# Masking attention scores inside the PSUM banks instead of into an SBUF tile

## The reference, cut to what matters

```python
qkv = silu(hidden_states @ qkv_w.T)              # q, k, v of every head
scores = einsum('bhnd,bhmd->bhnm', cq, ck) * diag_decay      # inside blocks of 32 tokens
intra = einsum('bhnm,bhmd->bhnd', scores, cv)
inter = einsum('bhnd,bhde->bhne', cq * q_decay, kv)          # from the blocks before
kv_next = kv * block_decay + einsum('bhnd,bhne->bhde', ck * k_decay, cv)
```

## Time and profile before

| | us |
|---|---|
| three runs: median (lowest to highest) | 1015.15 (1014.4 to 1015.38) |
| the profiled execution | 1015.99 |
| its span, first to last instruction | 1014.2 |
| TensorE busy in the span | 1000.2 |
| VectorE | 780.2 |
| ScalarE | 664.7 |
| GpSimd | 350.0 |

### The profile page before, as it was taken

How to read it: one execution, slowest core, us unless ns; L and a number is a source line. 1 busy time by engine, 2 the same in 40 slices (tenths; PEclk the granted TensorE clock), 3 DMA queues, 4 the chain that set the end, 5 groups by cost and what they waited for, 6 DMA issues and landing times.

```text
span 1014.2 us, 15712 instructions
## 1 busy us (share of the span) xinstructions
PE 1000.2 (99%) x5620; PEld 874.8 (86%) x5620; DVE 780.2 (77%) x1102; ACT 664.7 (66%) x1108; POOL 350.0 (35%) x329
## 2 busy tenths in 40 slices
PE   9999999999999999999999999999999999999996
PEld 7888988889888898889988898888978899888886
DVE  6777975887857976779757879579777797699885
ACT  6577754777467764677647774677637786477644
POOL 1353232341443223433323414342234323331462
PEclk9999999999999999999999999999999999999999
DMA  6021111110211111211111112111112111110402
GB/s 202 27 63 51 50 47 55 56 47 28 68 42 47 48 55 41 62 48 53 47 56 55 39 35 68 42 47 48 47 48 63 35 65 48 42 48 22 146 22 83
DMA packets 48814, 55.67 MB, mean 55 GB/s; under 512 B 4321, under 2 KB 40033, under 8 KB 48737
## 3 DMA queue, kind: packets, MB, share of 16 engines
q1 hardware_dynamic: 48736, 54.67, 17.0%
HBM read 52.56 MB, written 2.10 MB: 54 GB/s over the span
## 4 chain that ended last, share of the span: by engine, by line
PE 87%; DVE 6%; issue 2%; ACT 2%; POOL 1%; DMA 1%; SPq 0%; POOLq 0%; DVEq 0%; ACTq 0%
PE ps L1833 20%; PE ps L1834 19%; PE ps L1835 19%; PE ps L1827 9%; PE ps L1828 8%; PE ps L1829 8%; PE ps L1940 1%; PE ps L1925 1%; DVE wl L1048 1%; PE ps L1942 1%; DVE s L1029 1%; PE ps L1927 1%; ACT wh L387 1%; DVE yl L1029 1%; DVE acc L1148 1%
## 5 line engine op out<-in xcount | busy, mean ns | idle before, releaser
L1833 PE MATMUL ps<-xh,wh 128*128 128x512 f32 x658 | 261.8, 398 | 0.6 <-ACT stg L435 0.6
L1834 PE MATMUL ps<-xl,wh 128*128 128x512 f32 x658 | 257.2, 391 | 0.0
L1835 PE MATMUL ps<-xh,wl 128*128 128x512 f32 x658 | 256.1, 389 | 0.0
L1742 POOL TENSOR_TENSOR stage<-stage 128x512 f32<-128x512 f32 x61 | 87.4, 1432 | 331.4 <-DMA stage<-stream 331.3
L1762 POOL TENSOR_TENSOR sqacc<-sqacc,sq 128x512 f32<-128x512 f32 x64 | 92.3, 1442 | 271.1 <-ACT sq L546 271.1
L1029 DVE TENSOR_TENSOR wl<-stage,wh 128x1024 fp32r<-128x1024 f32 (+2 forms) x145 | 159.4, 1109 | 32.1 <-ACT wh L387 32.1
L387 ACT ACTIVATE wh<-stage 128x1024 fp32r<-128x1024 f32 (+2 forms) x145 | 122.1, 855 | 53.8 <-PE ps L1829 33.7
L1835 PEld LDWEIGHTS ps<-xh,wl 128*128 128x128 f32 x658 | 123.6, 188 | 26.6
L1833 PEld LDWEIGHTS ps<-xh,wh 128*128 128x128 f32 x658 | 123.5, 188 | 24.0 <-issue 1.0
L1834 PEld LDWEIGHTS ps<-xl,wh 128*128 128x128 f32 x658 | 123.9, 188 | 22.0
L1833 PE MATMUL ps<-wh,xh 128*128 128x256 f32 (+1 forms) x416 | 121.1, 291 | 0.0
(11 more groups left out here) (201 smaller groups left out, 2220.5 us busy)
## 6 DMA issues: line engine op xcount, KB each, us to landing
stage<-stream SPq DMA_DIRECT2D x61, 384.0 KB, 3.3
stage<-stream SPq DMA_DIRECT2D x42, 256.0 KB, 2.8
stage<-stream SPq DMA_DIRECT2D x63, 128.0 KB, 2.1
dec<-decay SPq DMA_DIRECT2D x32, 128.0 KB, 2.0
acc<-xt SPq DMA_DIRECT2D x8, 256.0 KB, 5.7
v<-x SPq DMA_DIRECT2D x8, 256.0 KB, 4.9
out<-acc SPq DMA_DIRECT2D x8, 256.0 KB, 2.1
sfull<-lora_router SPq DMA_DIRECT2D x1, 512.0 KB, 6.0
```

Source lines behind the costliest of these rows:

```text
L1742: nc.gpsimd.tensor_tensor(stage[:, s, 1:5:3, :], stage[:, s, 0:6:5, :], stage[:, s, 7:8, :].broadcast_to([P, 2, U]), ALU.add).then_inc(t_p ...
L1833: nc.tensor.matmul(dst, wt[0], mv_[0], start=start, stop=False, skip_group_check=True)
L1834: nc.tensor.matmul(dst, wt[0], mv_[1], start=False, stop=False, skip_group_check=True)
L1835: return nc.tensor.matmul(dst, wt[1], mv_[0], start=False, stop=stop, skip_group_check=True)
```

## The change

The masked scores no longer go to SBUF. `mask` takes the last 128 columns of each of the two banks, times the decays, into a new small SBUF tile `ssum`, and multiplies the first 384 columns in place, in the banks; for that the table of decays is lengthened from 256 to 384 columns by a copy of its first 128, on the host, and with it the tile `dec` and its load. `mask_sum` adds `ssum` onto columns 256 to 383 in the banks. `scores_hi` and `scores_lo` read the banks. `mask` waits for `s_full` of the half before (its `ssum` has been read), where it waited for `s_lo` of the half before (its `sfull` has been read). The tile `sfull` stays for other uses at the end of the kernel.

```diff
+        ssum = sb("ssum", [P, 2, P])
-        dec = sb("dec", [P, 2, SEQ])
+        dec = sb("dec", [P, 2, SC])
...
-                copy(sh[:, 2 * e:2 * e + 2, :], sfull[:, :, 0:SC]).then_inc(s_hi, 1)
+                copy(sh[:, 2 * e:2 * e + 2, :], att_banks(e, 0, SC)).then_inc(s_hi, 1)
...
             def mask(h, e):
                 i = 2 * h + e
-                dve.wait_ge(s_lo, i)
                 dve.wait_ge(sc_done, i + 1)
                 if e == 0:
                     dve.wait_ge(dec_in[h % 2], 16 * (h // 2 + 1))
-                part = att_banks(e, SEQ, W).rearrange("p b (a n) -> p b a n", a=2)
-                nc.vector.tensor_tensor(sfull[:, :, SEQ:W].rearrange("p b (a n) -> p b a n", a=2), part,
-                                        dec[:, h % 2, 0:P].unsqueeze(1).unsqueeze(1).broadcast_to([P, 2, 2, P]), ALU.mult)
-                nc.vector.tensor_tensor(sfull[:, :, 0:SEQ], att_banks(e, 0, SEQ),
-                                        dec[:, h % 2, :].unsqueeze(1).broadcast_to([P, 2, SEQ]), ALU.mult)\
+                dve.wait_ge(s_full, i)
+                nc.vector.tensor_tensor(ssum[:, :, :], att_banks(e, SC, W),
+                                        dec[:, h % 2, 0:P].unsqueeze(1).broadcast_to([P, 2, P]), ALU.mult)
+                nc.vector.tensor_tensor(att_banks(e, 0, SC), att_banks(e, 0, SC),
+                                        dec[:, h % 2, :].unsqueeze(1).broadcast_to([P, 2, SC]), ALU.mult)\
                     .then_inc(s_parts, 1)
...
-                nc.vector.tensor_tensor(sfull[:, :, SEQ:SC], sfull[:, :, SEQ:SC], sfull[:, :, SC:W], ALU.add)\
+                nc.vector.tensor_tensor(att_banks(e, SEQ, SC), att_banks(e, SEQ, SC), ssum[:, :, :], ALU.add)\
                     .then_inc(s_full, 1)
...
-                minus(sl[:, 2 * e:2 * e + 2, :], sfull[:, :, 0:SC], sh[:, 2 * e:2 * e + 2, :]).then_inc(s_lo, 1)
+                minus(sl[:, 2 * e:2 * e + 2, :], att_banks(e, 0, SC), sh[:, 2 * e:2 * e + 2, :]).then_inc(s_lo, 1)
...
-    return np.where(d >= 0, np.exp(-slope[:, None, None] * np.maximum(d, 0)), 0.0).astype(f)
+    table = np.where(d >= 0, np.exp(-slope[:, None, None] * np.maximum(d, 0)), 0.0).astype(f)
+    return np.concatenate([table, table[:, :, :P]], axis=2)
```

## The result

| | before | after |
|---|---|---|
| median of five runs, one job | 1015.38 (1014.4 to 1016.15) | 1011.2 (1010.33 to 1012.0) |
| the profiled execution, its span | 1015.99, 1014.2 | 1010.33, 1008.5 |

The ratio of the times is 0.9954, with a 95% interval of 0.9943 to 0.9966: faster by more than the 0.2% that a measurement can tell. The forecast was 1012.4 with a low end of 1011.3. Direction and place were right; the gain was half as large again as forecast (4.2 for 2.8 us), just past the end of the range, whose low end stood for a gain of 3.7.

What follows compares the result with a forecast made beforehand. TensorE bounds the kernel; only its gaps waiting for `yl` in `output`, 3.7 us, can return. Nine tenths of 3.1 at tiles 2 and 3, nothing at tile 4: 1015.15 - 2.8 = 1012.4 us, range 1011.3 to 1015.4.

Steps and rivals of the forecast that it cites:

- `sums_lo` gets in front of GpSimd: Second group's `output`: `sums_lo` moves from 146.28 to 145.63, before GpSimd's sum at 145.88, taking 0.95 instead of 2.04 us.
- the head start: VectorE before `output`: shorter `scores_lo` (0.54) and the missing wait (0.12) bring `y_low` 2 together 0.65 us earlier.
- the prediction's paragraph on the other stages: Other `output` stages: where GpSimd comes first by a hair, VectorE is still 0.4 us earlier, more than waits of 0.13 to 0.41.
- GpSimd's arrival does not move: GpSimd's sum in `output` hangs on weights made before `scores_lo`, so it cannot come before 145.88.
- The rule that spoke against it: Reads from banks: 65 ns more for each of two moved reads, head start 0.52, gain some 0.2 us smaller.
- the missing wait 0.12: At `mask`: no longer waiting for `s_lo` of the instruction just before lets it start 0.12 us earlier.
- nine tenths: Share taken of the 3.1 us lost before tiles 2 and 3 of the `output` stages: 2.8 us gain.
- the five small losses at tile 4: Five waits before tile 4 in `output`, some 0.11 us each, 0.6 us; they may stay, so nothing was taken.
- A wait costs its idle time less 0.16: Weight loads waiting for `yl` in `output`: 13 waits, 5.8 us idle, cost TensorE 3.7 us.
- the loss moves on to another tile: Rival in `output`: `y_low` 3 or 4 becomes the late one; half of the 3.7 us returns, 1013.3 us; chance 0.22.
- the contention at the scores stays: Rival at the score steps: bank operands still meet GpSimd, only 0.7 us gained, 1014.4 us; chance 0.07.
- The slow rival: `y_low` 2 or 3 caught behind GpSimd in all seven `output` stages, 1.0 us each, 1018.5 us; chance 0.11.

Runs made afterwards that it cites:

- r4: Kernel before, with GpSimd's sums of `qk1` held back from the second group on until `sums_lo` part A is made; 1012.74 us, ratio 0.9974.
- r6: Changed kernel with two unused 256-element VectorE multiplications before the masks ahead of `output`, from the second group on; 1016.03 us, ratio 0.9995.
- r3: Kernel before with the wide table, last 128 columns masked in the bank and `mask_sum` reading them there, `scores_lo` still reading `sfull`; 1015.23 us, ratio 1.0.
- r2: Changed kernel with `mask` waiting again for `s_lo` instead of `s_full` of the half before; 1011.91 us, ratio 0.9966.
- r7: Changed kernel with three unused 256-element VectorE multiplications before the masks ahead of `output`, from the second group on; 1018.92 us, ratio 1.0028.
- r8: Changed kernel with GpSimd's sums of `qk1` held back until `sums_lo` part A is made; 1009.88 us, ratio 0.9943.
- r10: Changed kernel with GpSimd's sums of `qk1` held back until `sums_lo` part A is made, timed a second time; 1011.26 us, ratio 0.9955.

## Why the prediction was right, and where its size failed

**Right: what bounds, and which place.** Only TensorE's gaps could come back, and those for `yl` in `output` were they: all 13 are gone, and no stage is above 21.79 us. r4 and r6 show the cause from both sides: two thirds of the gain come without the changed scores where the meeting is lifted otherwise, and all of it goes with them where VectorE is made as late as before. That `sums_lo` gets in front of GpSimd was less needed than the prediction's working suggests: in two of the changed kernel's seven stages it does not, and the head start alone closes the gap, as the prediction's paragraph on the other stages allowed. That GpSimd's arrival does not move held only to 0.4 us (+3.67 to +4.08).

**Right: prices of the steps.** The masks came out at 0.416 and 0.954 for the 0.43 and 0.95 that were taken, `mask_sum` at 0.427 for 0.43, `scores_lo` at 0.952 for 0.95 and ScalarE's copy at 0.804 for 0.81; VectorE's busy time fell to 765.4 where about 769 was expected (11 us were counted at the two steps and 11.7 came; the 768-column sums from `stage` fell from 62.5 to 57.1 besides, and the 1024-column ones rose from 67.3 to 68.8). The table's load cost nothing measurable (r3).

**The rule that spoke against it.** A bank as source added nothing to VectorE: `scores_lo` has a median of 0.951 from a bank and 0.958 from SBUF. The 120 cycles from PSUM against 58 from SBUF that the Trainium skill gives ("VectorE: DVE Perf Modes", the TRN2 errata) would be an estimated 65 ns more; they are not there, and the trace decides against this row. For the meetings the Trainium skill's page "SBUF — State Buffer", section "Who interferes with whom", states what the runs show: a VectorE instruction with two SBUF inputs contends with a GpSimd instruction that reads SBUF, one with at most one (outside the two-port modes) does not, and the order of issue decides who blocks. The trace agrees: `sums_lo` takes 0.95 when VectorE is 0.36 us ahead, 2.08 when it is 0.02 us behind (r2).

**Right in sum, wrong in parts: the head start.** 0.65 us was forecast, 0.67 came. But "the missing wait 0.12" was 0.20 (r2), and the shorter score steps gave 0.47, not 0.54: 0.54 is the difference in durations of `scores_lo`, and the start of the next instruction shows less (1.04 after it in r2, 1.53 before). That the two misses cancel is luck.

**Wrong: the sum.** The working had 5.8 - 13 x 0.16 = 3.7 us, of which 3.1 at tiles 2 and 3, "of which I take nine tenths, 2.8; tile 4, nothing". Measured in the stages: 4.48. So the step that failed is this sum, and with it the low end of the range, "all 3.7": the waits that it counts are the right ones, but their price was too low and some of the gap was left out. In the order of size:

- *Tile 4, 0.6 us.* "So the five small losses at tile 4 may stay": none did. `y_low` 4 ends at +9.24 to +9.30 in five stages and at +9.86 in the two in which GpSimd was still first at `sums_lo`, by 0.05 us; the first was well inside the interval that the prediction had worked out (150.9 to 151.8 on before's clock, that is +9.0 to +9.9), and even the late end cost no wait. That sum should have been carried to its end and weighed, not rounded to nothing.
- *The steps behind a wait, 0.5 us.* "A wait costs its idle time less 0.16" stops two steps too early. Over twelve steps from the one before the wait, the 13 cost 4.2 us and not 3.7, some 0.04 each more, since the matmuls just behind a wait follow one another at 0.232 and not at 0.227. After the wait of the earlier trace rows, whose last row starts at 146.75, the kernel before shows five such steps in 1.16 us, and then five in 1.13:

```profile
147.91 0.39 PE L1827 MATMUL ps<-wh,yh 128*128 128x512 f32 x1
...
149.04 0.39 PE L1829 MATMUL ps<-wh,yl 128*128 128x512 f32 x1
```

- *Nine tenths, 0.3 us.* The whole of it came.
- *A wait that was left out, 0.18 us.* In the first stage a weight load also waited for `wl` of `out_rows_lo`, and this row of before's list of waits has no counterpart after:

```profile
PEld ps L1827 <- DVE wl L1048: 0.3, 1, 0.3
```

So "that is all that VectorE takes from TensorE" was not so. This one goes with the execution, though: r1, the changed kernel again, has a wait of 0.2 us for the same tile. The four come to 1.6 us, and 2.8 + 1.6 = 4.4 of the 4.48. The medians say 3.9 to 4.2 (three jobs); the difference to 4.48 is within what the start and before's own meetings (see r3) do to an execution.

**The rivals.** That the loss moves on to another tile is refuted by the trace (no wait at any tile), and so is that the contention at the scores stays. The slow rival did not happen, but its mechanism and its price are real: r7's catches cost 1.1 us each for the 1.0 that was worked out. It decides at about one microsecond of VectorE; the changed kernel has that much between itself and a loss, and 0.67 us between itself and no gain.

## What to carry to other kernels

An edit that shortens an engine with 20% to spare is judged by what that engine meets next. Lay the two timelines over each other at one instruction, and ask who comes first at each meeting with GpSimd: two hundredths of a microsecond there are worth a whole one of that engine's time, though the bounding engine loses less of it, or nothing where there is slack. And count a wait of TensorE by the distance of starts over a dozen steps on both sides of it, not by its idle time, and count every wait of the list that ends on that engine, small ones too. One profile's count is still one execution's: kernels alike at this place differed by 0.9 us.

## What the runs showed of the hardware that was not expected

TensorE's granted clock rose between 4.3 and 11.0 us after the start, at other moments in two executions of one program, and its steps of 512 columns fell from 0.427 to 0.23 us with it; the clock column shows 1.00 also before. The first `output` stage began up to 2.3 us apart for one program (137.51 us in r8, 139.81 in r10, counted from the first matmul): more than r2's edit. A third of the gain, counted by starts, can hang on one semaphore wait of 0.20 us. And in the changed kernel's meetings at `sums_lo` the stretched instruction is each time the one that comes second: `sums_lo` first, it takes 0.95 and GpSimd's sum 1.75 to 1.98; GpSimd first, its sum takes 1.29 and `sums_lo` 2.06.
